# Twelve gapless token tiles instead of sixteen padded ones in a fused attention and expert kernel

## The chip, the cores and the metric

One core of one Trainium2 chip. The metric is the device time of one execution in microseconds (us).

## The reference

```python
h = patches @ W + b + pos_emb                  # 32 images x 16 patches, 768 -> 192
h = concatenate([h, txt], axis=1)              # 48 tokens an image, 1536 in all
h = h + attention(layernorm(h))                # 12 heads of 16, rotary, causal within an image
x = layernorm(h)
probs = softmax(x @ gate_w.T)                  # 8 experts; the two best, weights renormalised
pos = cumsum of one-hot choices; keep = pos < 480
buf[expert, pos] = x                           # 480 places for each expert
z = rmsnorm(2*buf) * norm_w[e]
y = buf + (silu(z @ w13g) * (z @ w13u)) @ w2   # hidden size 512
out = h + sum over the two choices of weight * y
```

## The kernel before, in words

The 32 images lie two to a tile of 128 partitions: 48 tokens in partitions 0 to 47, 48 in 64 to 111, the rest are gaps. So there are NT = 16 tiles, and a tile is also the unit of attention. The program is written by hand for each engine, with semaphores. It has three stages.

**Start.** PE multiplies the patches (L399). The first tiles' patch tokens are placed in h_all by eight small DMAs from ACT's queue (L576), the others through a buffer in HBM. DVE takes the mean and variance (`statistics`), POOL the reciprocal root (L978), DVE normalises (L748).

**Attention and routing.** `pipeline` runs `iteration(i, ...)` for i = 0 to 20 on PE, ACT, DVE and POOL; the middle ones stand in a hardware loop. Iteration i does, each engine in an order written out by hand: for tile i, the turn of the normalised rows (L414), the products for q and k (L455, L456) and for v (L459, L460), the rotation (DVE L837 to L842, sum on POOL L1001), the turn of q and k (L484), and ACT's copies into block-diagonal keys `kbd` (four of them, L635), queries (L637) and values (four, L646); for tile i-1 the scores with the mask added by a product (L440, L444), maximum and subtraction (DVE L824 to L830), exp (ACT L598), the turn of the probabilities (L476) and its copies (L610); for tile i-2 values (L425), division, turn (L451), output projection (L463), residual and second mean and variance (DVE L885 to L895), root on POOL (L1025); for tile i-3 the normalised row `x2` (DVE L815), its turn (L471), copies (L603), logits (L501, L502), square sum and a row of `rows` (ACT L623, L627; the buffer holds four tiles); every second iteration DVE makes the places and weights of two tiles (`r1`, `r2`, up to L879), and POOL scatters their rows into `slots` in HBM with two indirect DMAs a tile (L1037).

Then PE runs idle products to hold its clock: `stay_warm(34)`, a wait for all scattered rows, `stay_warm(20)` (L388).

**Experts.** For each of 8 experts SP loads w13 (L337, L339), w2 and the 480 rows `zs` (L346; two buffers). DVE scales the rows (L908 to L912), PE turns them (L511), PE makes four groups of up products of ten matmuls (L526 to L534), ACT does silu (L672), DVE the hidden product (L939), PE the down product (L549), DVE adds x (L951), ACT weighs (L681), POOL adds rows to the output by indirect DMA (L1053). For the next expert ACT casts the raw weights behind silu of m = 0 and m = 1, in its in-order queue:

```python
act.activation(sg[:, m % 2, :], bank[2 * (m % 2)][:, 0:CAP], ACT.Silu).then_inc(s_silu, 1)
if more and m < 2:
    split_high(e + 1, e0 + 1, 1 - par, m)     # waits for the raw weights of expert e + 1
```

## Time and profile before

| what | value |
|---|---|
| median of 3 runs | 337.92 us (335.21 to 338.64) |
| span of the profiled execution, first to last instruction | 336.1 us |
| PE, DVE, ACT, POOL busy | 285.1, 193.1, 157.0, 141.1 us |

The time of the profiled execution as a whole is not listed; its span is 1.8 us under the median, and that difference stands for what lies around the span. In the rows, L followed by a number is a line of the kernel; "start us, us" are start and duration; what stands in brackets is the idle time before an instruction and what ended it.

### The profile page before, as it was taken

Reading aid. Unit: us, or ns where it says so; the run is one execution under the profiler, and the core shown is the slowest. Engines: PE = TensorE matmul, PEld = TensorE weight load, DVE = VectorE, ACT = ScalarE, POOL = GpSimd, SP = SyncE. Lnnn points to the kernel's source line nnn. Section 1 sums busy time; section 2 is a strip of 40 time slices with the busy share of each in tenths; the row PEclk is TensorE's granted clock in tenths of the full one; section 3 lists DMA queues with packets and bytes.
Section 4 is the critical chain, followed back from the end, with each engine's and each line's share of the span. In section 5 each row is a group of like instructions: output and inputs, shape, how many; then the busy total and the mean of one; then the engine's idle time right before and its main releaser. Section 6 shows DMA issues by size and latency. Waiting matters only on the chain.

```text
span 336.1 us, 6386 instructions
## 1 busy us (share of the span) xinstructions
PE 285.1 (85%) x2009; PEld 229.2 (68%) x2009; DVE 193.1 (57%) x607; ACT 157.0 (47%) x442; POOL 141.1 (42%) x174
## 2 busy tenths in 40 slices
PE   7747899999999999988764999999999999999910
PEld 3624667777777777766642448998888897989900
DVE  3443586688788888884757036473737465463210
ACT  0023667777777777754733035445362535352110
POOL 9313233335545555542456600345251706153360
PEclk9975999999999999996965799999999999999985
DMA  7969700000000000050001190758475667561321
GB/s 245 279 158 324 267 3 0 2 1 12 21 15 25 9 19 19 19 126 19 19 20 38 49 250 4 177 97 222 100 173 140 133 139 134 164 100 11 33 29 15
DMA packets 24843, 30.33 MB, mean 90 GB/s; under 512 B 3345, under 2 KB 21559, under 8 KB 24691
## 3 DMA queue, kind: packets, MB, share of 16 engines
q1 hardware_dynamic: 18275, 21.45, 23.9%
q0 software_dynamic: 6288, 8.49, 12.2%
q8 instruction: 12, 0.20, 0.3%
q10 hardware_dynamic: 256, 0.10, 0.1%
q14 instruction: 12, 0.10, 0.1%
HBM read 19.61 MB, written 11.20 MB: 92 GB/s over the span
## 4 chain that ended last, share of the span: by engine, by line
PE 51%; ACT 14%; DMA 13%; DVE 8%; issue 7%; POOL 2%; ACTq 1%; SPq 0%; DVEq 0%; POOLq 0%
PE bank L549 12%; ACT kbd L635 7%; DMA zs<-slots 6%; PE bank L444 5%; PE bank L388 4%; PE bank L455 3%; PE bank L456 3%; DMA h_all<-ptok_sb 2%; ACT qT L637 2%; PE bank L533 2%; PE bank L440 2%; DMA slots<-rows,slot 2%; PE bank L534 2%; PE bank L527 2%; PE bank L530 2%
## 5 line engine op out<-in xcount | busy, mean ns | idle before, releaser
L1053 POOL DMA_INDIRECT out_rows<-yw,tok x32 | 51.1, 1596 | 85.6 <-ACT yw L681 78.3
L549 PE MATMUL bank<-w_sb,hT 128*120 128x192 f32 x256 | 43.4, 328 | 1.9 <-DVE hT L939 1.6
L549 PEld LDWEIGHTS bank<-w_sb,hT 128*120 128x120 f32 x256 | 41.4, 183 | 3.1 <-issue 3.0
L1001 POOL TENSOR_TENSOR qk<-rc,rs 128x192 f32<-128x192 f32 x32 | 18.7, 604 | 54.6 <-DVE rs L842 54.5
L939 DVE TENSOR_TENSOR hT<-sg,bank 128x480 f32<-128x480 f32 x32 | 20.8, 650 | 33.2 <-ACT sg L672 33.2
L1037 POOL DMA_INDIRECT slots<-rows,slot x32 | 32.4, 1012 | 9.5 <-issue 8.9
L672 ACT ACTIVATE sg<-bank 128x480 f32<-128x480 f32 x32 | 18.3, 572 | 31.5 <-PE bank L534 31.5
L681 ACT ACTIVATE yw<-yx,zs 120x192 f32<-120x192 f32 x32 | 12.8, 448 | 36.8 <-DVE yx L951 36.7
L635 ACT COPY kbd<-bank 32x288 f32<-32x288 f32 x64 | 24.9, 389 | 8.0 <-PE bank L484 6.8
L526 PE MATMUL bank<-z0h,wah 128*128 128x480 f32 x64 | 25.3, 395 | 0.2 <-ACT z0h L657 0.2
L533 PE MATMUL bank<-z,wbh 128*128 128x480 f32 x64 | 24.4, 381 | 0.3 <-DVE z L931 0.3
L530 PE MATMUL bank<-z0l,wah 128*128 128x480 f32 x64 | 24.4, 380 | 0.0
L527 PE MATMUL bank<-z0h,wal 128*128 128x480 f32 x64 | 24.3, 379 | 0.0
L534 PE MATMUL bank<-z,wbl 128*128 128x480 f32 x64 | 24.3, 379 | 0.0
L440 PE MATMUL bank<-maskb_sb,identb_sb 128*64 128x192 bf16 x96 | 13.1, 268 | 12.9 <-ACT qT L637 12.9
L444 PE MATMUL bank<-kbd,qT 128*64 128x192 f32 x192 | 23.2, 351 | 0.0
L388 PE MATMUL bank<-idle_sb 128*128 128x512 bf16 x65 | 18.2, 450 | 3.2 <-DVE rows L879 2.0
L824 DVE TENSOR_REDUCE mx<-bank 128x8 f32<-128x384 f32 x16 | 8.9, 557 | 19.7 <-PE bank L444 19.7
L951 DVE TENSOR_TENSOR yx<-bank,zs 120x384 f32<-120x384 f32 x16 | 8.9, 558 | 17.7 <-PE bank L549 17.7
L484 PE MATMUL bank<-ident_sb,qk 128*128 128x128 f32 x96 | 17.3, 297 | 1.7 <-POOL qk L1001 1.6
L598 ACT ACTIVATE pr<-sm 128x576 f32<-128x576 f32 x16 | 10.9, 683 | 15.1 <-DVE sm L830 15.1
L455 PE MATMUL bank<-wqkv_sb,xT 128*128 128x384 f32 x32 | 15.3, 565 | 1.8 <-ACT xT L587 1.8
(147 smaller groups left out, 661.1 us busy)
## 6 DMA issues: line engine op xcount, KB each, us to landing
rawa_sb<-in_w SPq DMA_DIRECT2D x8, 512.0 KB, 4.1
rawb_sb<-in_w SPq DMA_DIRECT2D x16, 256.0 KB, 5.0
w_sb<-in_w SPq DMA_DIRECT2D x8, 384.0 KB, 3.6
slots<-zero_sb POOLq DMA_DIRECT2D x1, 3030.0 KB, 14.0
zs<-slots SPq DMA_DIRECT2D x8, 378.8 KB, 4.9
patch_sb<-in_patches SPq DMA_DIRECT2D x1, 1152.0 KB, 6.7
out_rows<-h_all SPq DMA_DIRECT2D x2, 432.0 KB, 5.9
h_all<-in_txt SPq DMA_DIRECT2D x2, 384.0 KB, 8.6
```

Source lines behind the costliest of these rows:

```text
L388: pe.matmul(bank[0][:, :], idle_sb[:, 0:P], idle_sb[:, :], start=True, stop=True)
L444: mm = pe.matmul(bank[g // 2][lo:lo + HALF, cols], qT[:, q, g, lo:lo + HALF], kbd[:, q, two, g, :, :].rearrange("p a b -> p (a b)"), start ...
L455: pe.matmul(bank[4][:, 0:2 * D], xT0[:, :], wqkv0_sb[:, 0:2 * D], start=True, stop=False)
L526: pe.matmul(o, wah[:, par, cols], z0h[:, par, :], start=True, stop=False)
L527: pe.matmul(o, wal[:, par, cols], z0h[:, par, :], start=False, stop=False)
L530: pe.matmul(o, wah[:, par, cols], z0l[:, par, :], start=False, stop=False)
L533: pe.matmul(o, wbh[:, par, cols], z1[:, par, :], start=False, stop=False)
L534: mm = pe.matmul(o, wbl[:, par, cols], z1[:, par, :], start=False, stop=True)
L549: mm = pe.matmul(bank[6 + c // 2][0:CR, (c % 2) * D:(c % 2 + 1) * D], hT[:, m, c * CR:(c + 1) * CR], w2_sb[:, par, m, :], start=(m == 0), ...
L635: act.copy(kbd[32 * j:32 * j + 32, par, :, :, j, :], rows_k[:, :, :, 0:S]).then_inc(s_qkT, 1)
L1037: pool.indirect_dma_start(out=slots, out_offset=bass.IndirectOffsetOnAxis(ap=slot[:, quad // 2, 2 * q + k:2 * q + k + 1], axis=0), in_=row ...
L1053: pool.indirect_dma_start(out=out, out_offset=bass.IndirectOffsetOnAxis(ap=tok[:, e, c:c + 1], axis=0), in_=yw[:, c, :], in_offset=None, b ...
```

## The change

- h is cut into 12 tiles of 128 tokens without gaps. Attention still goes by 16 pairs of images: four groups of four pairs and three tiles (`front`, `projected`, `last_tile` say which tile step goes with pair j). Scores and v products pick columns of 48 tokens from q, k and x kept for a group of three tiles, in two buffers. The score banks and `pr` are doubled. Queries and keys are laid out for two heads by parity, so q and k need five turns a tile, not six. The scale goes into exp. The loop is unrolled.
- The first tile group's patch tokens are placed by three products with a 0/1 matrix; the others by eight DMAs from SP, with text from one `hinit` load.
- The router's logits come as 8 more columns of the qk product (through std1) and of the projection (with Wo times the centred gate, made once). The turn of x2, its copies and the logit products go; the mean square is worked out from the variance, so ACT's square and row copy go. DVE writes the normalised row straight into `rows`, which holds all tiles.
- Places and weights are made for three tiles at once (`BATCHES`); scatters are spread over the pairs (`SCATTERED`).
- SP fetches all eight experts' rows in a run behind the last scatter, and only then the weights of expert 1. DVE scales the next expert's rows after m = 0. ACT makes x times weight, DVE the weighted sum in one step per quarter; the last expert's down products finish quarter by quarter.
- POOL clears keys and slots; SP and ACT both load at the start.

```diff
+GROUPS = 4
+GT = 3
+GP = 4
+NT = GROUPS * GT
+NPAIR = GROUPS * GP
+GTOK = GT * P
...
+SCATTERED = {5: (0,), 6: (1,), 7: (2,), 9: (3,), 10: (4,), 11: (5,), 13: (6, 7), 14: (8,), 16: (9, 10, 11)}
+BATCHES = [(0, 1, 2), (3, 4, 5), (6, 7, 8), (9, 10), (11,)]
...
+def front(j):
+    i, g = j % GP, j // GP
+    first = GT * g
+    xt = {0: first + 2, 2: first + 3, 3: first + 4}.get(i)
+    qk = xt
+    qkt = {0: first + 1, 1: first + 2, 3: first + 3}.get(i)
+    keep = lambda t: t if t is not None and 0 <= t < NT else None
+    return keep(xt), keep(qk), keep(qkt)
+def projected(j):
+    i, g = j % GP, j // GP
+    t = {2: GT * g, 3: GT * g + 1, 0: GT * g - 1}.get(i)
+    return t if t is not None and 0 <= t < NT else None
+def last_tile(j):
+    return GT * (j // GP) + min(j % GP, GT - 1)
...
+            def scores(j):
+                pe.wait_ge(s_qT, last_tile(j) + 1)
+                pe.wait_ge(s_kbd, 4 * (last_tile(j) + 1))
+                if j >= 2:
+                    pe.wait_ge(s_pT, 2 * (j - 1))
+                bank = sc[j % 2]
+                g, at = (j // GP) % 2, (j % GP) * 2 * S
+                causal = maskb_sb[:, :].unsqueeze(1)
+                for lo in (0, HALF):
+                    pe.matmul(bank[lo:lo + HALF, 0, :].rearrange("p (g c) -> p g c", g=2)[:, :, 0:4 * S],
+                              identb_sb[:, lo:lo + HALF], causal.to_broadcast([P, 8, S]), start=True, stop=False)
+                for lo in (0, HALF):
+                    pe.matmul(bank[lo:lo + HALF, 1, 0:4 * S],
+                              identb_sb[:, lo:lo + HALF], causal.to_broadcast([P, 4, S]), start=True, stop=False)
+                for n in range(3):
+                    c0 = (n % 2) * 256
+                    for two in range(2):
+                        lo, cols = two * HALF, slice(at + two * S, at + (two + 1) * S)
+                        mm = pe.matmul(bank[lo:lo + S, n // 2, c0:c0 + 4 * S], qT[:, g, n, cols],
+                                       kbd[:, g, n // 2, :, cols], start=False, stop=(n >= 1))
+                mm.then_inc(s_sc, 1)
...
+            for j in range(NPAIR + 1):
+                i = j % GP
+                xt, qk, qkt = front(j)
+                back = j >= 1
+                if j == 0:
+                    pe.wait_ge(s_ptok, GROUPS)
+                    pe.wait_ge(s_gatec, 2)
+                if j < NPAIR:
+                    scores(j)
...
+                if back:
+                    turn_probs(j - 1)
+                if i == 2 and j < NPAIR:
+                    v_product(j)
+                if xt is not None:
+                    if i != 2 and back:
+                        pe.wait_ge(s_v, 4 * j)
+                    turn_x(xt, b7 if i == 2 else b5)
+                if qkt is not None:
+                    turn_qk(qkt)
+                if back:
+                    values(j - 1)
+                if qk is not None:
+                    if i == 2 and j >= GP:
+                        pe.wait_ge(s_posr, j // GP)
+                    qk_product(qk)
+                if i == 1:
+                    v_product(j)
+                    if j >= GP:
+                        pe.wait_ge(s_qT, GT * (j // GP + 1))
+                        positions(j // GP - 1, b4)
+                if j == NPAIR:
+                    positions(3, b4)
+                if back:
+                    turn_attention(j - 1)
+                if i in (0, 3) and j < NPAIR:
+                    v_product(j)
+                t = projected(j)
+                if t is not None:
+                    project(t)
+                if j == NPAIR:
+                    positions(4, b5)
...
+            stay_warm(34)
+            pe.wait_ge(s_disp, 32 * NT + 16)
+            stay_warm(20)
...
+            residual(0, 6)
+            residual(6, 9)
+            sp.wait_ge(s_disp, 32 * NT + 16)
+            for e in range(E):
+                sp.dma_start(zs[:, e, :, :],
+                             slots[e * CAP:(e + 1) * CAP, :].rearrange("(c p) r -> p c r", p=CR)).then_inc(s_zs[e], 16)
+                if e == 0:
+                    residual(9, NT)
+            for e in range(1, E):
+                sp.wait_ge(s_wl, 2 * e)
+                load_w13(e)
+                if e >= 2:
+                    sp.wait_ge(s_down, 2 * (e - 1))
+                    load_w2(e)
...
+            for j in range(NPAIR + 1):
+                i = j % GP
+                xt, qk, qkt = front(j)
+                back = j >= 1
...
+                if back:
+                    copy_probs(j - 1)
+                if xt is not None:
+                    copy_x(xt, b7 if i == 2 else b5)
+                if qkt is not None:
+                    copy_q(qkt)
+                if j < NPAIR:
+                    exponent(j)
+                if qkt is not None:
+                    copy_k(qkt)
+                if i in (1, 2) and j < NPAIR:
+                    copy_v(j)
+                if i == 1 and j >= GP:
+                    weight(j // GP - 1)
+                if j == NPAIR:
+                    weight(3)
+                if back:
+                    copy_attention(j - 1)
+                if i in (0, 3) and j < NPAIR:
+                    copy_v(j)
+                if j == NPAIR:
+                    weight(4)
...
+                    act.activation(sg[:, m % 2, :], up_bank[2 * (m % 2)][:, 0:CAP], ACT.Silu).then_inc(s_silu, 1)
+                    if e + 1 < E and m < 2:
+                        split_high(e + 1, m)
+                    if m == 2:
+                        weigh_x(e)
...
+            def rotate(t):
+                i = t % GT
+                dve.wait_ge(s_qkp, t + 1)
+                if t < GT:
+                    dve.wait_ge(s_rope[i], 16)
+                if t >= 1:
+                    dve.wait_ge(s_k, t)
+                    dve.wait_ge(s_q, t)
+                dve.wait_ge(s_std, (t + 1) if t < GT else GT + t // GT)
+                dve.tensor_scalar(gx[:, t, :], b4[:, 2 * D:2 * D + E], std1[:, t:t + 1], None, ALU.mult)
+                q2 = b4[:, 0:2 * D]
+                cos = rope_sb[:, i, 0, :].unsqueeze(1).to_broadcast([P, 2, D])
+                dve.tensor_tensor(rc[:, :].rearrange("p (a d) -> p a d", a=2), q2.rearrange("p (a d) -> p a d", a=2),
+                                  cos, ALU.mult)
+                pairs = q2.rearrange("p (a n two) -> p a n two", a=2, two=2)
+                rs4 = rs[:, :].rearrange("p (a n two) -> p a n two", a=2, two=2)
+                sin = rope_sb[:, i, 1, :].rearrange("p (n two) -> p n two", two=2)
+                for k in range(2):
+                    ins = dve.tensor_tensor(rs4[:, :, :, k], pairs[:, :, :, 1 - k],
+                                            sin[:, :, k].unsqueeze(1).to_broadcast([P, 2, D // 2]), ALU.mult)
+                ins.then_inc(s_rot, 1)
+            def shift(j):
+                dve.wait_ge(s_sc, j + 1)
+                if j >= 1:
+                    dve.wait_ge(s_exp, j)
+                both = sc[j % 2][:, :, :].rearrange("p a c -> p (a c)")
+                three = both[:, 0:768].rearrange("p (g c) -> p g c", c=256)[:, :, 0:4 * S]
+                four = three.rearrange("p g (h k) -> p g h k", k=S)
+                dve.tensor_reduce(mx[:, :].rearrange("p (g h) -> p g h", g=3), four, AX.X, ALU.max).then_inc(s_mx, 1)
+                dve.wait_ge(s_mx, j + 1)
+                dve.tensor_tensor(sm[:, :].rearrange("p (g h k) -> p g h k", g=3, k=S), four,
+                                  mx[:, :].rearrange("p (g h) -> p g h", g=3).unsqueeze(3).to_broadcast([P, 3, 4, S]),
+                                  ALU.subtract).then_inc(s_sh, 1)
...
+            def residual(t):
+                dve.wait_ge(s_proj, t + 1)
+                ht = h_all[:, t, :]
+                dve.tensor_tensor(ht, b6[:, 0:D], ht, ALU.add).then_inc(s_res, 1)
+                dve.tensor_tensor(lg[:, t, :], b6[:, D:D + E], gx[:, t, :], ALU.add).then_inc(s_lg, 1)
+                dve.wait_ge(s_res, t + 1)
+                link(dve.bn_stats(st2[:, :], ht))
+                link(dve.bn_aggr(mv2[:, :], st2[:, :]))
+                if t >= 2:
+                    dve.wait_ge(s_pw, t - 1)
+                link(dve.tensor_scalar(vp[:, t % 2, 0:1], mv2[:, 1:2], LN_EPS, None, ALU.add))
+                link(dve.reciprocal(iv[:, :], vp[:, t % 2, 0:1]))
+                dve.tensor_scalar(vp[:, t % 2, 1:2], iv[:, :], mv2[:, 1:2], RMS_EPS / 4, ALU.mult, ALU.add).then_inc(s_vp2, 1)
+                dve.wait_ge(s_lg, t + 1)
+                dve.max(top[:, t, :], lg[:, t, :]).then_inc(s_top, 1)
+            def norm2(t):
+                dve.wait_ge(s_top, t + 1)
+                dve.max_index(choice[:, t, :], top[:, t, :], lg[:, t, :]).then_inc(s_choice, 1)
+                dve.wait_ge(s_pw, t + 1)
+                dve.tensor_scalar(rows[:, t, 0:D], h_all[:, t, :], mv2[:, 0:1], rows[:, t, RSTD_COL:RSTD_COL + 1],
+                                  ALU.subtract, ALU.mult).then_inc(s_row, 1)
...
+            patch_tokens(0, b7)
+            dve.wait_ge(s_h0, 16)
+            for t in range(GT):
+                dve.wait_ge(s_placed, t + 1)
+                dve.tensor_tensor(h_all[:, t, :], sc[t // 2][:, t % 2, 0:D], h_all[:, t, :], ALU.add).then_inc(s_hin, 1)
+                dve.wait_ge(s_hin, t + 1)
+                statistics((t,), t)
+                if t == 1:
+                    dve.wait_ge(s_rstd1, 1)
+                    norm1(0)
+            dve.memset(pr[:, :, :, :], 0.0).then_inc(s_ready, 1)
+            for t in range(GT):
+                deviation((t,), t)
+            dve.wait_ge(s_std, GT)
+            norm1(1)
+            rotate(0)
+            patch_tokens(1, sc[1][:, 1, :])
+            dve.wait_ge(s_mask, 16)
+            dve.wait_ge(s_ident, 16)
+            dve.tensor_copy(maskb_sb[:, :], mask_sb[:, :])
+            dve.tensor_copy(identb_sb[:, :], ident_sb[:, :]).then_inc(s_maskb, 1)
+            patch_tokens(2, b6)
+            rotate(1)
+            patch_tokens(3, sc[0][:, 0, :])
+            norm1(2)
+            dve.wait_ge(s_gmean, 1)
+            for n in range(2):
+                w = (P, D1)[n]
+                dve.tensor_tensor(gatec_sb[0:w, n, :], gate_sb[0:w, n, :], sc[0][0:w, 1, 0:E], ALU.subtract).then_inc(s_gatec, 1)
+            dve.wait_ge(s_order, 16)
+            dve.tensor_copy(before_sb[:, :], orderf_sb[:, :])
+            for j in range(NPAIR + 1):
+                i, g = j % GP, j // GP
+                xt, qk, qkt = front(j)
+                if j < NPAIR:
+                    shift(j)
+                t = projected(j - 1)
+                if t is not None:
+                    norm2(t)
+                if i == 1 and j >= GP:
+                    route(g - 1)
+                if j == NPAIR:
+                    route(3)
+                if i == 1 and g + 1 < GROUPS:
+                    if g == 0:
+                        dve.wait_ge(s_ptok_in, 16 * (GTOK // S))
+                    statistics(range(GT * (g + 1), GT * (g + 2)), GT + g)
+                    deviation(range(GT * (g + 1), GT * (g + 2)), GT + g)
+                if j >= 1:
+                    divide(j - 1)
+                nxt = front(j + 1)[0]
+                if nxt is not None:
+                    if nxt % GT == 0:
+                        dve.wait_ge(s_std, GT + nxt // GT)
+                    norm1(nxt)
+                if i == 1 and j >= GP:
+                    assign(g - 1, b4)
+                if j == NPAIR:
+                    assign(3, b4)
+                if qk is not None:
+                    rotate(qk)
+                t = projected(j)
+                if t is not None:
+                    residual(t)
+                if j == NPAIR:
+                    norm2(t)
+                    route(4)
+                    assign(4, b5)
...
+            for j in range(NPAIR + 1):
+                i, g = j % GP, j // GP
+                xt, qk, qkt = front(j)
+                if i == 1 and g + 1 < GROUPS:
+                    rstd(range(GT * (g + 1), GT * (g + 2)), GT + g)
+                if qk is not None:
+                    rotated(qk)
+                t = projected(j)
+                if t is not None:
+                    power2(t)
+                if j == GP + 1:
+                    pool.wait_ge(s_disp, 16)
+                for t in SCATTERED.get(j, ()):
+                    scatter(t)
...
```

## Rows read from the trace of the kernel before

**Rows 1.** busy of PE, PEld, DVE, ACT, POOL by stretch; clock, DMA share, GB/s

```profile
96.83:113.99 17.16, 16.01 (x159) 12.61 (x159) 14.29 (x58) 12.23 (x45) 9.18 (x17) 1.00 0.06 20
...
214.54:306.23 91.69, 89.81 (x482) 81.04 (x481) 51.28 (x78) 41.49 (x74) 38.41 (x24) 1.00 0.62 135
```

**Rows 2.** timeline of PE: scores of first and last tile

```profile
30.26 0.37 PE L440 MATMUL bank<-maskb_sb,identb_sb 128*64 128x192 bf16 x2 [1.16 <-ACT qT L637]
...
163.49 0.27 PE L440 MATMUL bank<-maskb_sb,identb_sb 128*64 128x192 bf16 x2 [1.09 <-ACT qT L637]
```

**Rows 3.** chain of waits inside one iteration: start, us, what

```profile
107.88 0.33 PE bank L444 x4
...
109.39 0.65 PE bank L455 x2
```

**Rows 4.** timeline of DVE in one iteration

```profile
100.48 0.56 DVE L824 TENSOR_REDUCE mx<-bank 128x8 f32<-128x384 f32 x1 [0.48 <-PE bank L444]
...
102.13 0.56 DVE L837 TENSOR_TENSOR rc<-bank,rope_sb 128x384 f32<-128x384 f32 x1
...
105.09 0.36 DVE L888 BATCH_NORM_STATS2 st<-h_all 128x6 f32 x1
...
105.56 0.18 DVE L891 BATCH_NORM_AGGREGATE mv<-st 128x2 f32<-128x6 f32 x1
```

**Rows 5.** groups by line and form, whole span

```profile
L635 ACT COPY kbd<-bank 32x288 f32<-32x288 f32 x64 | 24.9, 389 | 8.0 <-PE bank L484 6.8
...
L598 ACT ACTIVATE pr<-sm 128x576 f32<-128x576 f32 x16 | 10.9, 683 | 15.1 <-DVE sm L830 15.1
...
L978 POOL TENSOR_TENSOR rstd<-ve,small_sb 128x3 f32<-128x3 f32 x1 | 0.9, 870 | 2.8 <-DVE ve L731 2.8
...
L1001 POOL TENSOR_TENSOR qk<-rc,rs 128x192 f32<-128x192 f32 x32 | 18.7, 604 | 54.6 <-DVE rs L842 54.5
```

**Rows 6.** PE by stretch: busy, granted clock, DMA share, GB/s

```profile
151.00:152.00 1.00, 0.00 (x0) 0.50 0.00 0
...
158.00:159.00 1.00, 1.00 (x8) 1.00 0.00 0
```

**Rows 7.** timeline of iteration 14: ACT's row copy, then PE

```profile
149.94 0.35 ACT L627 COPY rows<-x 128x192 f32<-128x192 f32 x1 [1.90 <-DMA slots<-rows,slot]
...
152.39 0.37 PE L440 MATMUL bank<-maskb_sb,identb_sb 128*64 128x192 bf16 x2 [2.55 <-ACT qT L637]
```

**Rows 8.** timeline behind the last tile

```profile
181.41 0.17 DVE L796 TENSOR_TENSOR pos<-bank,count 128x16 f32<-128x16 f32 x1 [0.32 <-PE bank L498]
...
183.35 14.28 PE L388 MATMUL bank<-idle_sb 128*128 128x512 bf16 x54 [1.99 <-DVE rows L879]
...
190.70 0.97 POOL L1037 DMA_INDIRECT slots<-rows,slot  x1 [0.30 <-issue]
...
193.02 0.87 SPq L346 DMA_DIRECT2D zs<-slots  x2
```

**Rows 9.** all engines by stretch, after the last scatter

```profile
195.00:196.00 1.00, 1.00 (x7) 0.43 (x5) 0.00 (x0) 0.00 (x0) 0.00 (x0) 1.00 1.12 272
```

**Rows 10.** timeline of ACT: expert 1's raw weights

```profile
203.12 1.05 ACT L665 CAST wah<-rawa_sb 128x1024 fp32r<-128x1024 f32 x1 [0.22 <-DMA rawb_sb<-in_w]
```

**Rows 11.** timeline of the start

```profile
6.32 2.19 PE L399 MATMUL bank<-tokw_sb,patch_sb 128*128 128x192 f32 x12 [1.19 <-DMA patch_sb<-in_patches]
...
18.72 0.38 DVE L748 TENSOR_SCALAR xn<-h_all,mv,rstd 128x192 f32<-128x192 f32 x1 [0.24 <-POOL rstd L978]
```

**Rows 12.** timeline of the experts

```profile
206.48 0.38 PE L526 MATMUL bank<-z0h,wah 128*128 128x480 f32 x1
...
229.35 0.51 PE L526 MATMUL bank<-z0h,wah 128*128 128x480 f32 x1
...
236.36 0.17 DVE L908 CAST tok<-zs 120x4 f32 x1 [1.02 <-DMA zs<-slots]
```

**Rows 13.** timeline of the end

```profile
326.77 1.58 POOL L1053 DMA_INDIRECT out_rows<-yw,tok  x1 [0.30 <-issue]
```

1324 lines of the change are left out of this document (605 added, 719 removed).

## The prediction

> **What bounds the kernel now.** I first read the busy time by stretch of two attention iterations in the middle and of six experts [rows 1]. Two iterations take 17.16, of which PE is busy 16.0, DVE 14.3, ACT 12.2: 8.58 a tile, with PE nearly full and DVE close behind, since its steps wait for one another. Six experts take 91.7, of which PE has 89.8: there only PE counts. Then I read the places where the work is not steady. From the first scores to those of the last tile, 15 iterations, 133.2 pass [rows 2]; 15 x 8.58 is 128.7, so 4.5 are lost. They are lost in iteration 14: ACT copies a row into a `rows` buffer that a scatter still reads (1.90 of waiting), PE stands still 2.55 and then runs its products longer [rows 7], with the granted clock at 0.50 (1.2 GHz) until about 158, when it is back at 1.00 (2.4 GHz) [rows 6]. Behind the last tile there are 16.2 from the last places (181.41) to the first turn of the experts (183.35 + 14.28 = 197.6), half of it POOL's indirect DMAs, the last issued at 190.70, and idle products on PE [rows 8].
>
> **The start.** Tokens of the first tiles come by products, not by eight small DMAs: before, the patch product starts at 6.32 and the first normalised rows at 18.72 [rows 11]. Now both queues load at once, which puts some 600 KB (three tiles of 98, two biases of 96, the identity's 64 and small ones) beside the first 960; at the 272 GB/s of a full queue [rows 9] that is 2, of which I take 1.5: product at 7.8. Then 2.2 for it, 0.4, products 0.5, DVE's sum and statistics 1.1, POOL's power 0.6, and the second tile's sum and statistics, 1.1, which stand before norm1(0): 13.5. But the qk product waits for a memset of `pr` behind a third tile: 16.4. From there PE has 9.9 of work at full clock (two qk products, three patch products, turns), some at half clock after its idle time: 12.4, so scores(0) at 29.3, 1.0 earlier. The 6 won by the placing are mostly spent on patch products that now stand in front of the loop.
>
> **The loop.** PE's work for four pairs and three tiles: four 128*64 instructions of the scores take 0.33, two of a 392-column product 0.65 [rows 3]. A pair is scores 1.25, turn of probabilities 0.7, values 0.8, v 0.65, turn 0.35: 3.75. A tile is turn 0.3, qk 1.3, five turns 0.6, projection 0.7: 2.9. Together 24, against 34.3 for four iterations before. ACT has 19.3. So the bound is DVE, with what its in-order queue waits for. An independent DVE instruction starts 0.09 before the end of the one ahead, one that waits for its predecessor 0.11 behind it (0.36 becomes 0.47) [rows 4]. By that: `shift` is two dependent operations of 576 elements, 0.77 each: 1.54, where four pieces took 1.65 [rows 4]; `divide` 0.54; `norm1` 0.29; `rotate` 1.15; `residual` 1.8; `norm2` 0.57; three tiles' statistics 1.4 and a wait for POOL's power of three (0.87) [rows 5] with the deviation 1.3; `route` 1.0; `assign` 2.4, twelve small steps, mostly dependent.
>
> In a pair with i = 0 or 3 there is a ring: shift 1.54, exp 0.68 and four key copies of 0.41 on ACT [rows 5], ACT's copy of the attention behind them 0.45, projection 0.7, with four handovers of 0.1 to 0.2: residual begins 5.35 after shift, ends at 7.15; DVE itself would be free at 4.1. So the logits' removal is not what counts there, ACT's order is. For i = 2 there are no key copies: 6.45. For i = 1 DVE has everything: 1.54 + 0.57 + 1.0 + 2.7 + 0.54 + 0.29 + 2.4 = 9.0. A group is 7.15 + 9.0 + 6.45 + 7.15 = 29.75. In i = 1 PE has nothing from the positions until the division: some 3.0, more than the 2.55 after which it ran at half clock [rows 6, 7]. After such a fall PE ran at half clock for some 5; PE has 5.8 of slack in a group, and I add 1.5. First group, without routing: 26.6; two at 31.25; the last up to shift(15), without statistics: 7.15 + 6.0 + 6.4 = 19.6. From shift(0), 30.7, that is 139.4. Before, shift(15) came 1.5 behind the last scores, at 165.0: 25.6 earlier. The 4.5 of iteration 14 are in it: `rows` holds all tiles, and no one waits for its scatter.
>
> POOL's four sums (1.6 a tile, from 0.60 for 192 elements [rows 5]), power and two scatters of 1.3 a pair are beside this. The eight zeroing and placing DMAs land before DVE asks in pair 1; if late, that costs what they are late.
>
> **Behind the last tile.** Residual(10) ends 6.35 after shift(15); then DVE has norm2, route, divide, assign, residual(11): POOL's power is at 13.1, and only then, in POOL's order, the scatters of tiles 9 and 10, 5.2; tile 11's places are there at 17.1. Its two go until 21.1, the last lands at 22.2 (as 190.70 became 193.02 [rows 8]). PE starts its 34 idle products at 14.6, at half clock as before; 54 of them took 14.28 [rows 8], so the turn is at 28.7 or later, while the data would allow 26.8. Before: 197.6 - 165.0 = 32.6. So 3.9 less; turn at 168.1.
>
> **Experts.** Rows fetched ahead help: the second expert, whose rows were there, took 229.35 - 214.54 = 14.81; six of 91.7 / 6 = 15.28 save 0.47 each, 2.8, since no one waits for rows as in [rows 12]. But SP now queues six more loads, 379 KB each, ahead of expert 1's raw weights. Before, those were ready 203.12 - 193.02 = 10.1 after the first fetch, just in time [rows 8, 10]. At 272 GB/s, with the engines' share at 1.12 [rows 9], 2.27 MB are 8.3 more: 18.4. ACT's cast waits for them in front of silu of m = 1, DVE's product waits for that, and PE's group m = 3, whose banks it frees: 1.04 + 0.57 + 0.65 + handovers = 2.6 later, 21.0 after the fetch. Without the wait m = 3 would begin 6.5 (turn behind the fetch) + 8.9 (206.48 - 197.6 [rows 12]) = 15.4 after it. So PE stalls 5.6, and some 5 us follow at half clock: 2.5. DVE now waits for the adds of the expert before, with the next hidden products queued behind it; ACT had that wait before, and POOL's four adds of 1.6 plus 0.3 are over in the first half of an expert, so it costs nothing. Sum of the stage: 5.6 + 2.5 - 2.8 = +5.3.
>
> The table of the Trainium skill, DMA: Bandwidth & Descriptors, section Specifications, gives 358 GB/s from HBM for a core; by it the six loads would be 6.3, the stall 3.6 and the sum 2 lower. The row has 272 for rows of 812 bytes, so I stay with it.
>
> **The end.** The first quarter of the last down product is ready after 7 of 16 parts and not after 12, and one step replaces two; the last of POOL's four (326.77 [rows 13]) comes 2.3 earlier.
>
> **Sum.** -25.6 (with the 1.0 of the start) - 3.9 + 5.3 - 2.3 = -26.5: span 336.1 - 26.5 = 309.6, and with the 1.8 between span and median 311.4.
>
> **Rivals.** (a) *No stall in expert 1*: its weights overtake, or the fetches are faster. Speaks for it: the rate rests on one stretch, with rows of 812 bytes, and the order in the queue on one arrival [rows 9, 10]; against: behind two fetches the weights did come last, and no earlier than their turn. -8.1: 303. Chance 0.17.
>
> (b) *Products with 48 columns are not run side by side.* Before, scores used halves of 64 columns, and four instructions took the time of two full ones [rows 3]; none with 48 is in the trace. At double cost scores (+1.0) and v (+0.65) make PE's group 30.6, which with low clock now sets 34: +12, 324. Chance 0.1, and no more, since the halves still begin at partitions 0 and 64, as in the rows.
> The Trainium skill, TensorEngine Tiling (Array Packing), sections Tiling Modes and Restrictions, asks only that the active columns fit a tile of 64; by it this case would not come, and no row here shows 48.
>
> (c) *Slower: the clock falls in every pair.* PE's load in the loop drops from 93% to 80% and its waits for ACT's order come in each pair, not once a group. If a fall like that of iteration 14 comes 16 times, PE works at 1.2 GHz for about 5.3 of every 7; its 96 of loop work then take some 150 and the ring waits for each of its products too: +33, 344. It decides when more than two thirds of the loop are at 0.50: PE alone then needs 144, and with the stall nothing is left. Against it: iterations at 93% kept 1.00 [rows 1], and pairs 0, 2 and 3 (PE 6.0 to 6.6 of 6.5 to 7.2) are as dense. Chance 0.08.
>
> (d) *DVE's waits are shorter than the ring says* (ACT done before the exp, no falls): group 26.5, another -14: 297. Chance 0.08. That some gain is lost in the start (PE cold for all of it, late placement) and in waits I don't see: +20, 331: 0.07.
>
> **How the numbers follow.** Forecast 0.5, with 304 to 318 as its own spread. The range, 298 to 331, leaves out (c) and the far edge of (d) and of the last case. 1% (3.4) is about what can be told from no change. Faster by more: 0.5 + 0.17 + 0.1 + 0.08 and half of the last case, less a margin for what is wrong in all of it at once: 0.86. Within: 0.05. Slower: 0.09.
>
> **What would show it.** First scores near 29; shift to shift 7.2, 9.0, 6.5, 7.2; DVE's largest wait for the projection; granted clock at 0.5 for some us after each pair with i = 1, none elsewhere; no wait on a scatter; turn near 168; ACT's first cast for expert 1 ended by the raw weights' DMA, idle some 10, and PE silent before m = 3 of expert 0; later experts at 14.8. Wrong if the group takes over 33, if PE is at 0.5 in most of the loop, or if raw weights come within 13 of the fetch.

## The result and the profile after

The changed kernel takes 318.42 us (median of 4 runs, 318.17 to 322.33), the kernel before 338.28 beside it; the ratio is 0.945 (95% interval 0.940 to 0.951). I had said 311.4, with 298 to 331 as range. The profiled execution has a span of 316.1, 20.0 less than before, where I had 26.5 less. The saving arrives as follows. "Shift" is the start of DVE's maximum of a pair (L872), "turn" PE's turn of an expert's rows (L574).

| stretch | my term | measured | missed by |
|---|---|---|---|
| start to first shift | 30.7 | 34.2 | +3.5 |
| first group of four pairs | 26.6 | 27.5 | +0.9 |
| groups two and three | 2 x 31.25 | 31.0 + 30.9 | -0.6 |
| then to shift(15) | 19.6 | 19.3 | -0.3 |
| shift(15) to the first turn | 28.7 | 30.2 | +1.5 |
| first turn to second (11.05 before) | +8.1 | 21.6, that is +10.5 | +2.4 |
| six experts behind it (91.15 before) | -2.8 | 88.3, that is -2.9 | -0.1 |
| last turn to last add (26.96 before), and behind it | -2.3 | 24.25 and 0.5 less behind | -0.9 |

The last column gives +6.4 of the 6.5 between 309.6 and 316.1; the rest is rounding. Most of the saving is the loop: from shift(0) to shift(15) it is 108.7, where it was 132.0, and PE's busy time in it 97.5, where it was 119.4. No kernel here takes back one part of the change alone, so how much of this belongs to the tiles without gaps and how much to the router's columns is not shown.

*The start*, from the timeline of all engines, where [rows 11] stood before:

```profile
8.72 2.97 PE L374 MATMUL bank<-tokw_sb,early 128*128 128x192 f32 x12 [2.25 <-DMA tokw_sb<-in_tokw]
...
15.47 0.37 DVE L840 TENSOR_SCALAR xn<-h_all,mv,rstd 128x192 f32<-128x192 f32 x1
...
17.18 1.34 DVE L967 MEMSET pr<- 128x1536 f32 x1 [0.27 <-issue]
...
18.77 1.64 PE L388 MATMUL bank<-wqkg_sb,xT 128*128 128x392 f32 x2 [2.12 <-DVE pr L967]
...
24.57 5.18 POOL L1137 MEMSET blank<- 128x6090 f32 x1
...
25.21 4.58 DVE L976 CAST maskb_sb<-mask_sb 128x48 bf16<-128x48 f32 x1
25.30 4.55 DVE L977 CAST identb_sb<-ident_sb 128x128 bf16<-128x128 f32 x1
...
32.80 0.35 PE L423 MATMUL scores<-maskb_sb,identb_sb 128*64 128x384 bf16 x2 [0.74 <-DVE gatec_sb L985]
```

The patches' product starts at 8.7 (I had 7.8) and takes 2.97, from 10 on at half clock (I had 2.2). The normalised rows come at 15.5, the qk product starts at 18.8, released by the memset of `pr` as I had said, and the first scores at 32.8. Two conversions to bf16 take 4.6 us each beside POOL's memset; before they took 0.28 (a wider mask) and 0.21. They overlap, from 25.21 to 29.85, so they hold DVE for 4.6 in all and not for twice that.

*The loop.* The chain of waits in a pair with i = 0; the lines left out are PE's too, and from 84.0 to 98.3 there is no gap between them:

```profile
91.14 0.28 PE scores L423 x2
...
91.50 0.97 PE scores L432 x12
...
94.88 0.86 PE bank L388 x2
...
96.61 0.79 PE bank L410 x8
...
97.94 0.35 PE bank L471 x2
98.29 0.02 issue
```

So here PE is the limit: 7.14 from pair to pair, the sum of its own work. Where [rows 3] had 0.33 for four score instructions of 64 columns, twelve of 48 take 0.97. In the pair with i = 1 it is DVE and its wait for POOL (timeline of DVE), and PE's clock falls behind it (stretches: PE, PEld, DVE, ACT and POOL busy, granted clock, DMA share, GB/s):

```profile
99.91 0.74 DVE L872 TENSOR_REDUCE mx<-scores 128x12 f32<-128x576 f32 x1
...
104.97 0.16 DVE L835 TENSOR_TENSOR std<-ve,rstd 128x3 f32<-128x3 f32 x1 [0.97 <-POOL rstd L1095]
105.05 0.23 DVE L881 RECIPROCAL rden<-bank 128x12 f32<-128x12 f32 x1
...
109.00 0.76 DVE L872 TENSOR_REDUCE mx<-scores 128x12 f32<-128x576 f32 x1 [0.97 <-PE scores L432]
```

```profile
102.00:104.00 2.00, 0.97 (x17) 0.55 (x13) 1.86 (x11) 1.88 (x7) 0.00 (x0) 1.00 0.59 190
104.00:106.00 2.00, 0.28 (x2) 0.23 (x2) 1.00 (x6) 0.78 (x4) 0.85 (x1) 0.89 0.34 109
106.00:108.00 2.00, 2.00 (x14) 1.15 (x14) 1.73 (x12) 0.37 (x2) 0.00 (x0) 0.50 0.00 0
```

PE has 0.97 of 2 us, then 0.28; the granted clock goes from 1.00 (2.4 GHz) to 0.50 (1.2 GHz), back at 1.00 by 110; the scores run at half clock, and DVE waits 0.97 for them. Shift to shift the four pairs of group two take 7.14 (i = 0), 9.04 (1), 7.69 (2) and 7.14 (3).

*Behind the last tile*, POOL and PE (timelines):

```profile
157.74 0.70 POOL L1120 TENSOR_TENSOR rows<-vp,small_sb 128x2 f32<-128x2 f32 x1 [6.36 <-DVE vp L908]
...
165.26 0.98 POOL L1127 DMA_INDIRECT slots<-rows,slot  x1 [0.30 <-issue]
```

```profile
159.44 0.19 PE L479 MATMUL bank<-hots,before_sb 128*128 128x8 bf16 x1 [3.43 <-DVE hots L930]
...
159.52 13.80 PE L370 MATMUL scores<-idle_sb 128*128 128x512 bf16 x54
173.16 0.99 PE L574 MATMUL bank<-ident_sb,blank 120*128 120x120 f32 x8
...
190.96 0.77 PE L589 MATMUL scores<-z0h,wah 128*128 128x480 f32 x1 [8.80 <-DVE blank L1068]
```

The idle products run from 159.5 until the turn without a gap. The last line is the stall: PE stands 8.8 us in front of group m = 3 of expert 0. SP and ACT tell why; the line of [rows 10] had a wait of 0.22 at this place:

```profile
167.63 0.37 SPq L355 DMA_DIRECT2D keys<-slots  x1
...
168.54 7.61 SPq L355 DMA_DIRECT2D keys<-slots  x7
176.19 1.68 SPq L333 DMA_DIRECT2D early<-in_w  x1
```

```profile
177.82 0.57 ACT L782 ACTIVATE blank<-scores 128x480 f32<-128x480 f32 x1 [1.53 <-PE scores L597]
188.70 1.04 ACT L762 CAST wah<-early 128x1024 fp32r<-128x1024 f32 x1 [10.30 <-DMA early<-in_w]
```

The raw weights of expert 1 are issued behind eight fetches, of which the last seven keep SP itself busy for 7.6 us, and ACT has them 21.1 after the first fetch (167.63 to 188.70).

### The profile page after: what moved, and what is told of

It reads as the page before. It is cut to its first block, busy times and chain, and to the rows that moved or that the text cites. A ratio compares the mean times of both kernels' runs of the same rounds, so it can differ in the third digit from the quotient of the medians.

```text
span 316.1 us, 5261 instructions
## 1 busy us (share of the span) xinstructions
PE 266.9 (84%) x1882; PEld 206.6 (65%) x1882; DVE 178.9 (57%) x523; ACT 126.8 (40%) x333; POOL 123.0 (39%) x131
## 4 chain that ended last, share of the span: by engine, by line
PE 52%; issue 6%; DMA 4%; DVE 4%; SPq 3%; POOL 3%; ACT 2%; POOLq 0%; ACTq 0%
PE bank L605 13%; PE scores L589 4%; PE scores L590 4%; PE scores L593 4%; PE scores L597 4%; PE scores L596 4%; DMA early<-in_w 3%; PE scores L432 3%; SPq L355 2%; PE bank L458 2%; PE bank L410 2%; PE bank L574 2%; PE scores L439 2%; PE bank L388 2%; PE bank L470 2%
## 5 line engine op out<-in xcount | busy, mean ns | idle before, releaser
L1167 POOL DMA_INDIRECT out_rows<-blank,tok x32 | 55.4, 1730 | 87.3 <-DVE blank L1055 80.3
L1068 DVE TENSOR_TENSOR blank<-blank,scores 128x480 f32<-128x480 f32 x32 | 20.9, 654 | 39.0 <-ACT blank L782 39.0
L605 PE MATMUL bank<-w_sb,blank 128*120 128x192 f32 x256 | 42.9, 326 | 0.0
L605 PEld LDWEIGHTS bank<-w_sb,blank 128*120 128x120 f32 x256 | 41.4, 183 | 0.1
L589 PE MATMUL scores<-z0h,wah 128*128 128x480 f32 x64 | 26.0, 406 | 9.2 <-DVE blank L1068 8.8
L596 PE MATMUL scores<-z,wbh 128*128 128x480 f32 x64 | 24.5, 383 | 0.3 <-DVE z L1051 0.3
L593 PE MATMUL scores<-z0l,wah 128*128 128x480 f32 x64 | 24.7, 386 | 0.0
L590 PE MATMUL scores<-z0h,wal 128*128 128x480 f32 x64 | 24.7, 386 | 0.0
L597 PE MATMUL scores<-z,wbl 128*128 128x480 f32 x64 | 24.6, 384 | 0.0
L432 PE MATMUL scores<-keys,qT 128*48 128x192 f32 x192 | 20.3, 351 | 0.0
L589 PEld LDWEIGHTS scores<-z0h,wah 128*128 128x128 f32 x64 | 12.3, 192 | 11.4 <-DVE blank L1068 9.2
L458 PEld LDWEIGHTS bank<-vbd,pT 128*64 128x64 f32 x384 | 13.1, 143 | 5.0 <-ACT pT L694 4.2
L872 DVE TENSOR_REDUCE mx<-scores 128x12 f32<-128x576 f32 x16 | 11.9, 746 | 6.6 <-PE scores L432 6.6
## 6 DMA issues: line engine op xcount, KB each, us to landing
slots<-blank POOLq DMA_DIRECT2D x1, 3045.0 KB, 14.6
```

The lines of the kernel that those rows point to most:

```text
L432: mm = pe.matmul(bank[lo:lo + S, n // 2, c0:c0 + 4 * S], qT[:, g, n, cols], kbd[:, g, n // 2, :, cols], start=False, stop=(n >= 1))
L458: mm = pe.matmul(b6[lo:lo + HALF, p * w:(p + 1) * w], pT[:, j % 2, p, lo:lo + HALF], vbd[:, j % 2, two, p, :, :].rearrange("p a b -> p (a ...
L589: pe.matmul(o, wah[:, par, cols], z0h[:, par, :], start=True, stop=False)
L590: pe.matmul(o, wal[:, par, cols], z0h[:, par, :], start=False, stop=False)
L593: pe.matmul(o, wah[:, par, cols], z0l[:, par, :], start=False, stop=False)
L596: pe.matmul(o, wbh[:, par, cols], z1[:, par, :], start=False, stop=False)
```

## The experiments

Twelve kernels ran, in three groups of four, each group on one chip. The kernel before took 341.7 beside the first four, 338.5 beside the next four and 339.8 beside the last four (medians), so kernels of different groups are compared by their ratio to it; the changed kernel's is 0.945 (0.940 to 0.951). The changed kernel did not run again beside them, and the ratios have an uncertainty of their own: three kernels that lose the stall took 309.4, 309.5 and 309.5, and their ratios are 0.901, 0.912 and 0.915. So kernels of different groups are told apart only where they differ by more than about 1.5%. Single profiles differ too. The last stretch, from shift(14) to shift(15), is 6.2 in four of them and 6.7 to 7.9 in the others, as PE's clock is at 1.00 or falls to 0.50 in it, and where the start is unchanged, the first shift comes at 33.5 to 35.7. Differences of 1.5 to 2 between single profiles can come from this alone, so I read single stretches.

**Weights first.**

```diff
             for e in range(E):
                 sp.dma_start(zs[:, e, :, :], ...)
                 if e == 0:
                     residual(9, NT)
+                if e == 1:
+                    sp.wait_ge(s_wl, 2)
+                    load_w13(1)
             for e in range(1, E):
-                sp.wait_ge(s_wl, 2 * e)
-                load_w13(e)
+                if e >= 2:
+                    sp.wait_ge(s_wl, 2 * e)
+                    load_w13(e)
...
```

> SyncE issues the raw weights of expert 1 right behind the rows of experts 0 and 1, ahead of the other six experts' rows; nothing else is changed. If the weights came late because they stood behind six fetches in the queue, they land some 10 us after the first fetch and not 21; TensorE's idle time of 8.8 us in front of group m = 3 of expert 0 goes, and the half clock behind it: 10 us less, 308. If the fetches as a whole are the limit and the wait only moves (to the rows of expert 1 or the weights of expert 2), it is 0 to 3 less, 316 to 318.

309.4 us, ratio 0.901 (0.894 to 0.909). SP, then ACT:

```profile
169.50 0.37 SPq L355 DMA_DIRECT2D keys<-slots  x1
...
170.95 0.62 SPq L333 DMA_DIRECT2D early<-in_w  x1
...
172.79 9.53 SPq L355 DMA_DIRECT2D keys<-slots  x6
```

```profile
179.81 0.57 ACT L786 ACTIVATE blank<-scores 128x480 f32<-128x480 f32 x1 [1.54 <-PE scores L601]
180.89 1.05 ACT L766 CAST wah<-early 128x1024 fp32r<-128x1024 f32 x1 [0.50 <-DMA early<-in_w]
```

The weights land 11.4 after the first fetch, ACT waits 0.5, and from the first to the second turn it is 11.0 as before the change, not 21.6. The six experts' rows behind cost nothing later: the next turns follow at 14.7. The place in the queue was the cause, and 10.6 is its price in the profiles; the medians, from different chips, give 9.0.

**Rows in turn.** Rows of expert e + 1 behind the raw weights of e.

```diff
-            for e in range(E):
+            def fetch(e):
                 sp.dma_start(zs[:, e, :, :], ...)
-                if e == 0:
-                    residual(9, NT)
+
+            fetch(0)
+            residual(9, NT)
+            fetch(1)
             for e in range(1, E):
                 sp.wait_ge(s_wl, 2 * e)
                 load_w13(e)
+                if e + 1 < E:
+                    fetch(e + 1)
```

> SyncE fetches the rows of expert e + 1 behind the raw weights of expert e, two experts ahead of use at the start and one later, no longer all at once. The stall in expert 0 goes as with the weights first: 10 us less. If fetching ahead is what took the experts from 15.3 to 14.7 us, they go back towards 15.3 where rows come late, +0.5 each for six: 311. If rows one expert ahead are early enough, they stay at 14.7: 308.

309.5, ratio 0.912 (0.905 to 0.920), and all pitches between turns from the second on are 14.7 to 14.8. So one expert ahead is enough; fetching all at once brought only the stall.

**PE less, ACT less.** Two kernels that leave work out, to see who sets the pairs with i = 0 and 3: the first leaves out the causal mask from pair 2 on, the second two of the four key copies of every tile.

```diff
-                for lo in (0, HALF):
+                for lo in (0, HALF) if j < 2 else ():      # so for both loops of mask products
...
-                                       kbd[:, g, n // 2, :, cols], start=False, stop=(n >= 1))
+                                       kbd[:, g, n // 2, :, cols], start=(j >= 2), stop=(j >= 2 or n >= 1))
```

```diff
-                for n in range(4):
+                for n in range(2):                         # key copies on ACT; each now counts for two
```

> Leaves out the causal mask from pair 2 on (its four products of 0.36 us together a pair), so the output is not the reference's; only TensorE has less to do. If TensorE itself sets the pairs with i = 0 and 3 (its chain there has no gaps), these go from 7.14 to 6.8 us, about ten pairs of 14 in all: 3 to 4 us less. If the ring that I predicted (shift, exp, key copies, attention copy, projection, residual) sets them, the period stays at 7.14 and the time is the same within 1 us.

> Leaves out two of the four key copies of every tile on ScalarE (0.36 to 0.41 us each; half of the keys stay zero, so the output is not the reference's). If the ring that I predicted sets the pairs with i = 0 and 3, ScalarE's copy of the attention comes 0.75 us earlier and each of these pairs shortens by about that: 5 to 7 us less. If TensorE sets them: the same within 1 us.

Without the mask the period goes from 7.14 to 6.91, without two key copies it stays at 7.13 to 7.14 in five of the six pairs (the first of them, pair 3, took 7.44): PE sets it, not the ring. 0.36 of work less gave 0.23, since the scores that now stand first took 1.11 and not 0.97 (kernel without the mask, chain of waits; PE without a gap again):

```profile
85.30 1.11 PE scores L432 x12
86.41 0.80 PE scores L439 x6
...
90.54 0.79 PE bank L410 x8
```

The ring, then, is 6.9 long or less. ACT's copies did count in pair 13, which has 5.29 without two of them and 5.92 to 5.94 in every other kernel but the one with filled waits. As whole times both are no gain: 320.8 and 321.0, ratios 0.938 (0.930 to 0.946) and 0.940 (0.934 to 0.946). Six pairs without the mask at 0.23 are 1.4, and not the 3 to 4 that I had expected of ten pairs. The pairs with i = 1 and 2 of groups two and three together took 0.5 to 0.7 more than in the changed kernel (8.7 + 8.8 for 9.0 + 7.7, and 8.6 + 8.5 for 9.1 + 7.5), at half clock for longer, and the last pair 0.5 more; the profile's mean clock is 0.894 for 0.915. From shift(0) to shift(15) it is 108.6 for 108.7: what the lighter PE won was lost in the half clock of other pairs.

**Division early.**

```diff
+                if i == 1 and j >= 1:
+                    divide(j - 1)
                 if i == 1 and g + 1 < GROUPS:
                     statistics(...); deviation(...)
-                if j >= 1:
+                if i != 1 and j >= 1:
                     divide(j - 1)
```

> In pairs with i = 1 the division goes ahead of the statistics of three tiles (it stood behind them, 2.1 us late, with TensorE idle for 2.8 and at half clock behind it). If VectorE's own work sets this pair (9.0 us of it), the pair keeps 8.1 to 9.0 and only the half clock behind it goes: 1 us for each of three groups, in all 2 to 4 less. If the division was what all waited for, the pair loses the whole 2.1 and the fall: 7 to 8 less. If the fall has another cause: nothing changes but the place of TensorE's wait, within 1 us.

316.5, ratio 0.925 (0.917 to 0.933), beside 320.8 and 321.0 of the two kernels above on the same chip; the intervals nearly touch or just overlap. The pair with i = 1 takes 8.16 (9.04), and a whole group 30.2 (31.0). It is not the 2.1 by which the division had been late: DVE itself needs about 8.1. The fall of the clock went later, into a pair with i = 3 in each of these groups (7.54 and 7.99), and did not go away.

**The wait filled.** Ten idle products where PE waits for the division; first in every pair with i = 1, then, on top of the weights first, in pairs 5 and 9 alone.

```diff
+                if i == 1 and back:          # then: if j in (5, 9):
+                    for _ in range(10):
+                        pe.matmul(sc[(j - 1) % 2][:, 0, :], idle_sb[:, 0:P], idle_sb[:, :], ...)
                 if back:
                     turn_attention(j - 1)
```

> Ten idle products of 0.22 us stand in pairs with i = 1 ahead of the attention's turn, where TensorE waits 2.8 us for the division. If the half clock behind this wait comes from the idle time, it goes, and the pairs with i = 2 take 7.14 and not 7.5 to 7.7 (8.4 on another chip): 0.5 to 1 less in each of three groups, 1.5 to 3 in all. If the clock falls anyway, nothing or slightly slower.

> On top of the kernel with the weights first, ten idle products in pairs 5 and 9 alone (with them in 1 and 13 too, two groups shortened by 1.6 each and the first and last pairs lost as much). By the clock's part: pairs with i = 1 8.0 and with i = 2 7.1 in groups two and three, 3.2 less than the kernel with the weights first. If what is won comes back as a lower clock in the last pairs, 0 to 1.

The first: 320.8, ratio 0.947 (0.938 to 0.956), no gain. Groups two and three took 29.4 each (31.0), but pair 1 took 8.5 (7.6) and pair 13 6.8 (5.9), where there was less to fill, and the last pair and expert 0 ran longer (7.9 for 6.2, 22.7 for 21.6). The second: 306.0, ratio 0.905 (0.899 to 0.910). The weights alone gave 0.901 on another chip; in the same group as this one, with a start edit that changed nothing (below), they gave 309.5 and 0.915 (0.910 to 0.921). So the filling is worth some 3.5 in that group, where I had expected 3.2. In its profile the pair with i = 1 is DVE's alone, and the clock stays up (timeline of DVE, stretches):

```profile
97.62 0.74 DVE L879 TENSOR_REDUCE mx<-scores 128x12 f32<-128x576 f32 x1
...
105.67 0.75 DVE L879 TENSOR_REDUCE mx<-scores 128x12 f32<-128x576 f32 x1
```

```profile
97.62:105.67 8.05, 7.34 (x84) 4.62 (x83) 6.57 (x36) 4.84 (x15) 1.57 (x2) 1.00 0.24 76
```

From 97.62 to 105.67, 8.05, DVE goes from step to step, but for 0.97 in which it waits for POOL's power. So the pair's 9.04 were 8.05 of DVE and 0.97 of scores at half clock; with some 0.5 in the next pair the clock costs about 1.5 a group (31.0 became 29.4). The wait does not bring the fall every time: among the 18 groups two and three of the nine kernels with the late division and nothing filled, one (pairs 4 to 7 of the kernel with the zeros first, below) kept 1.00 and took 29.4 as well; the group behind it lost more, 32.3. All four filled groups kept 1.00.

**Behind the last tile.** Tile 9's scatters ahead of tile 11's power; then 24 idle products for 34 as well.

```diff
-SCATTERED = {..., 16: (9, 10, 11)}
+SCATTERED = {..., 16: (10, 11)}
...
+                if j == NPAIR:
+                    scatter(9)
                 if t is not None:
                     power2(t)
...
-            stay_warm(34)
+            stay_warm(24)
```

> POOL issues the two scatters of tile 9 ahead of tile 11's power and not behind it, into its idle time of 6.4 us. The last scatter is then issued some 2.6 us earlier and SyncE's first fetch follows. If TensorE's 54 idle products (13.8 us without a gap, from the places of tile 10 on) set the turn of the first rows, the time stays the same within 0.5 us: rows wait for TensorE. If the scatters set it, 2.6 less.

> As the kernel with tile 9's scatters moved, and 24 idle products instead of 34 ahead of the wait for the scatters. By both theories the turn now comes with the data, 2.2 to 2.6 us earlier; if this gains and the other does not, the idle products were the limit. If the granted clock is not up by the turn, the expert stage loses what is won, 0.

318.6, ratio 0.942 (0.934 to 0.949), and 318.8, ratio 0.942 (0.934 to 0.950): neither moved. PE in the first, then in the second:

```profile
161.80 14.29 PE L370 MATMUL scores<-idle_sb 128*128 128x512 bf16 x52 [0.24 <-issue]
175.92 0.99 PE L574 MATMUL bank<-ident_sb,blank 120*128 120x120 f32 x8
```

```profile
161.22 11.13 PE L370 MATMUL scores<-idle_sb 128*128 128x512 bf16 x43 [0.24 <-issue]
172.83 1.04 PE L574 MATMUL bank<-ident_sb,blank 120*128 120x120 f32 x8 [0.48 <-DVE blank L1033]
```

The first expectation was wrong in its premise, that the last scatter would come 2.6 earlier: the first fetch is 24.6 behind shift(15) in this kernel and 24.7 in the changed one, since POOL's power now stood behind the scatters and tile 11's places came later; its last scatter waited 1.4 for them. The idle products did set the turn (32.3 behind shift(15)), and with ten fewer it waited for DVE's scaled rows instead (28.9). But that won nothing either: the second turn came 26.7 and 27.4 behind the first fetch (at 194.9 and 195.0), as it came 27.1 behind it in the changed kernel (at 194.8), for the stall ends with the weights, whenever it began. As long as the stall was there, nothing between the first fetch and it counted.

**The start.** On top of the weights first: POOL's memset of `blank` behind the second tile's sums; in another kernel `pr` zeroed while DVE waits for the identity.

```diff
             rotated(0)
-            pool.memset(zero_sb, 0.0)
             rotated(1)
+            pool.memset(zero_sb, 0.0)
...
+            dve.memset(pr[:, :, :, :], 0.0).then_inc(s_ready, 1)
             dve.wait_ge(s_ident, 16)
...
-            dve.memset(pr[:, :, :, :], 0.0).then_inc(s_ready, 1)
             for t in range(GT):
```

> On top of the kernel with the weights first, POOL zeroes its big buffer (5.2 us) behind the second tile's key and query sums, no longer between the two, where VectorE's two conversions to bf16 took 4.6 us each beside it. If POOL's memset holds them up, they take 0.2 to 0.3 now, as before the change. If, as I read the trace, TensorE's own work sets the start (its products run on without a gap but 0.7), the first shift comes at most 0.7 earlier; if the conversions were on the path, 3 to 4 earlier.

> On top of the kernel with the weights first, VectorE zeroes pr (1.34 us) while it waits for the identity, not behind the third tile. The first qk product (18.77, ended by this memset) then waits only for its own input, 17.2: the first shift comes 1.5 earlier and so does all else, 1.5 less than the kernel with the weights first. Rival: TensorE's products behind it run at half clock longer, and it gives 0.5 or less.

The first: 309.5, ratio 0.915 (0.910 to 0.921), no gain. Timeline:

```profile
16.09 1.65 PE L392 MATMUL bank<-wqkg_sb,xT 128*128 128x392 f32 x2 [2.37 <-DVE pr L971]
...
23.14 0.18 DVE L980 CAST maskb_sb<-mask_sb 128x48 bf16<-128x48 f32 x1
23.23 0.22 DVE L981 CAST identb_sb<-ident_sb 128x128 bf16<-128x128 f32 x1
...
30.76 5.17 POOL L1142 MEMSET blank<- 128x6090 f32 x1
```

The conversions take 0.18 and 0.22. From the qk product to the first shift it is 16.1, against 15.5 in the changed kernel: 4.6 us less in which DVE is held took nothing off PE's chain. The second: 306.1, ratio 0.904 (0.898 to 0.910), 3 better than the first. Timeline:

```profile
15.68 0.37 DVE L845 TENSOR_SCALAR xn<-h_all,mv,rstd 128x192 f32<-128x192 f32 x1
...
17.21 0.90 PE L392 MATMUL bank<-wqkg_sb,xT 128*128 128x392 f32 x2 [0.60 <-ACT xT L662]
```

From the normalised rows to the qk product it is 1.5, where it is 3.3 in the changed kernel and in the first of these two: the memset was on the path, and 1.8 is what it cost there. The qk product runs 0.90 and 0.82 where it took 1.64 and 1.51, and the first shift is 14.8 behind it. I don't count this second gain as the edit's: in the kernel with everything together, which has the same edit, the product took 1.65 again, and the first shift was 15.9 behind it. Nor do the 3 us between the two medians come from the start as far as their profiles show. The first shift is at 32.0 and at 32.2, since the patches' product began at 8.5 here and at 7.2 there; the profiled spans part in the loop (108.7 and 110.7) and between shift(15) and the turn (30.8 and 32.2), in both of which PE's clock differs.

**Together**: weights first, memset later, zeros first, division early, six idle products in pairs 5 and 9, and 24 for 34 behind the last tile; the scatter stays where it was.

> Everything together: weights first, POOL's memset later, pr zeroed first, the division ahead of the statistics, six idle products in pairs 5 and 9, 24 idle products ahead of the turn and not 34. If the parts add, 8.5 to 10 for the weights, 1.5 for the start, 3 to 4 for the loop, 0.4 for the turn: 303 to 304 where the changed kernel has 318.4. If the clock's falls move elsewhere, 306 to 308.

303.9, ratio 0.900 (0.893 to 0.906); lowest run 299.95, span of the profiled one 297.8. Groups two and three take 28.6 (8.16, 6.20, 7.13 and 7.14), with the clock at 1.00 throughout the loop. The profile is of the shortest of the six runs, with a mean clock of 0.946; the other five have 0.917 to 0.938, so this need not hold for each of them. The turn is 28.8 behind shift(15) (30.2 in the changed kernel, 29.3 to 32.3 in the other profiles with 34 idle products). It is what I expected if the parts add, 303 to 304. Its interval lies wholly below the changed kernel's (0.940 to 0.951); the quotient of the two ratios is 0.952. Against two of its parts (0.904 and 0.905) the intervals overlap, so what the early division, the moved memset and the fewer idle products add to those two is not shown.

## Why the prediction was right or wrong

**Right in sign, in the range, 7.0 too low.** The forecast's own spread was 304 to 318; 318.4 lies just outside it.

**The start** is the step that failed most, 3.5. "Product at 7.8", "2.2 for it", "norm1(0): 13.5", "qk 16.4" became 8.7, 3.0, 15.5, 18.8: 0.9 of loading, 0.8 for the patches' product, which ran at 0.50 from 10 on where I took full clock, the rest mainly the placing products, at 0.50 too. Then 12.9 for PE became 14.0. That the memset of `pr` releases the qk product was right, and shown by its move. The conversions beside POOL's memset I had not seen; they are hidden. Where the start is unchanged, the first shift lies between 33.5 and 35.7 in ten profiles, so 3.5 is a size with 1 either way.

**The loop** came out within 0.1 in all (+0.9, -0.6 and -0.3), and that is luck: the reason was wrong and the misses cancel. "The bound is DVE" with a ring of 7.15 is refuted for i = 0 and 3: less work on PE shortened the pair, less on ACT did not. I had PE at 3.75 + 2.9 = 6.65 for such a pair; it is 7.14, since qk is 1.52 and not 1.3, the projection 0.88 for 0.7, v 0.79 for 0.65, the turn of the probabilities 0.81 for 0.7 and scores 1.33 for 1.25, while the other turns together are 0.26 less. The 0.65 of [rows 3] is for 384 columns, not 392, but the 8 columns are not it: of the qk product's two halves one takes 0.66, and only the first 0.86. Why it does is open. The ring is at most 6.9. The 7.15 of the ring and the measured 7.14 agree by chance, and this hid that the mechanism was another. For i = 1 "DVE has everything: 9.0" was right in kind: it is 8.05, and 0.97 of the clock's price falls into this pair, so that the 9.04 agree by chance. For i = 2 I had 6.45; with the clock up it is 7.11, and 6.20 only in the kernel that also divides early. 1.5 a group for the clock was right: 1.6. So behind the group's 31.25 for 31.0 stand one pair forecast 0.95 too long and one 0.66 too short.

**Behind the last tile**, 1.5: tile 11's power at 14.8 behind shift(15) and not 13.1, so PE's idle products start at 16.6 and not 14.6. The order of causes was right: the last scatter is issued 22.3 behind (21.1), and idle products of 13.8 set the turn.

**Experts.** The mechanism of the stall was right and is shown; its size was not: the weights were ready at 21.1, not 18.4. I took the 272 GB/s of [rows 9], one stretch of 1 us, for the whole queue. During the fetches of rows the trace shows 215 to 226 GB/s at a DMA share of 1.07 to 1.14 (stretches of 4 us from 172 to 184); at that rate the six loads more, 2.34 MB, take 10.3 to 10.9 by estimate and not 8.3, which is most of the 2.7. They also hold SP, so that the weights are issued 8.6 after the first fetch; whether that costs anything beside the rate is not shown, as the DMA share does not drop. PE reached the stall 0.9 sooner than I had (14.5 behind the first fetch for 15.4), so it stood 8.8 (5.6), and it lost 1.6 by half clock (2.5). The table of the Trainium skill, DMA: Bandwidth & Descriptors, section Specifications, has 358 GB/s; for these rows the trace is far below. The 2.8 from rows ahead came (2.9), but one expert ahead would have done.

**The end**: 2.7 for 2.3, and 0.5 less behind it.

**Rivals.** (a) No stall: refuted. (b) 48 columns side by side: twelve in 0.97 where 64 columns had 3 x 0.33 [rows 3]; refuted as a rival. The Trainium skill, TensorEngine Tiling (Array Packing), section Restrictions, asks of their number only that it fits the tile; the trace agrees. (c) A fall in every pair: refuted, in the changed kernel's profile pairs with i = 0 and 3 keep 1.00. (d) Shorter waits: refuted, the group takes 31.0, not 26.5.

## What to carry to other kernels

A load for the next stage stands in the same queue as a prefetch: issue what is needed first, and prefetch only as far ahead as it is used; here the order of one call in SP's list was worth 9 to 10.6 us, about half of what the whole change won. Two bounds that come out close in the working (a ring of 7.15, PE at 6.65) with terms that are uncertain by 0.1 to 0.2 each don't say which one holds: a kernel with a little less of each tells them apart. An early finish in front of a stall that ends with a transfer is worth nothing, so remove the stall first and measure the rest after.

## What the runs showed of the hardware

- Conversions of f32 to bf16 on DVE, 128x48 and 128x128, took 4.58 and 4.55 us beside a memset of POOL from 24.57 to 29.75 and ended at 29.79 and 29.85; without it they took 0.18 and 0.22. With `pr` zeroed first, when the memset ran to 26.8, they took 3.9 and ended as it ended. DVE's sum from PSUM at 24.93 took its usual 0.36 beside it. By the Trainium skill, SBUF — State Buffer, section SBUF: two separate sides, DVE in some modes and POOL exclude each other for a whole instruction; the trace agrees.
- The transfers of 812-byte rows ran at 215 to 226 GB/s; at the start the two queues together reached 357 to 411 GB/s (stretches of 2 us from 10 to 16).
- SP's issue of a fetch takes 0.4 to 0.8 us, and 1.6 to 1.8 from the sixth of the eight on (changed kernel, 167.6 to 176.2).
- Ten idle products (2.2 us) in the wait of 2.8 kept PE at 2.4 GHz in all four groups that had them; of 18 without them one kept it. With the early division and six of them the clock stayed at 1.00 through the loop, and with the early division alone (one profile each) it fell. In pair 14 of the changed kernel the clock took no notice of the waits; in the kernel with the weights first PE was busy as long in the same place, 1.44 of 3 us, and the clock fell to 0.50 at its end (the changed kernel, then the other). What decides there stays open.

```profile
137.70:140.70 3.00, 1.44 (x28) 1.06 (x25) 1.17 (x3) 1.89 (x7) 2.39 (x3) 1.00 0.17 61
```

```profile
139.20:142.20 3.00, 1.44 (x25) 1.06 (x22) 1.14 (x3) 1.89 (x7) 2.39 (x3) 0.95 0.20 69
```
